# Tables in three parts, residuals ahead of low splits, earlier x1 loads: one change to a deformable-convolution and attention kernel

## The reference

```python
out = relu(bn(conv1x1(x, w1), g1, b1, m1, v1))               # 1024 -> 256 channels
offset = conv3x3(out, w_off, b_off)                          # 18 offsets a pixel
out = relu(bn(deform_conv3x3(out, offset, w2), g2, b2, m2, v2))  # 9 taps, 4 corners each
x = relu(bn(conv1x1(out, w3), g3, b3, m3, v3) + x)           # 256 -> 1024, residual
...
t, p, g = Wt @ x, Wp @ x, Wg @ x                             # 1024 -> 512 channels each
att = [sum(alpha_o * p**o * g) for o in 0, 1, 2]             # one number an image and order
y = sum(att_o * alpha_o * t**o)
z = Wz @ y                                                   # 512 -> 1024 channels
return (z - mean(z)) * rsqrt(var(z) + eps) * gn_w + gn_b + x
```

## Time and profile before

| what | us |
|---|---|
| median of 3 runs | 2401.27 |
| the three runs | 2401.27, 2420.3, 2396.08 |
| the profiled execution | 2397.66 |
| its span, first to last instruction | 2395.8 |
| busy: PE, PEld | 2252.3 (94%), 1860.6 (78%) |
| busy: DVE, ACT, POOL | 1575.6 (66%), 1248.5 (52%), 764.8 (32%) |
| DMA over the span | 684.76 MB, mean 286 GB/s |
| TensorE's mean granted clock | 0.974 |

### The profile page before, as it was taken

How to read it: one execution, slowest core, us unless ns; L and a number is a source line. 1 busy time by engine, 2 the same in 40 slices (tenths; PEclk the granted TensorE clock), 3 DMA queues, 4 the chain that set the end, 5 groups by cost and what they waited for, 6 DMA issues and landing times.

```text
span 2395.8 us, 29891 instructions
## 1 busy us (share of the span) xinstructions
PE 2252.3 (94%) x10252; PEld 1860.6 (78%) x10252; DVE 1575.6 (66%) x3177; ACT 1248.5 (52%) x2432; POOL 764.8 (32%) x706
## 2 busy tenths in 40 slices
PE   8999999998989999999999999999999999999960
PEld 6888887877867788888888887888778878887840
DVE  4213127667467888898888988898783324467774
ACT  6444444343455565666565655566553324456664
POOL 0100013324114554565567665766560000000000
PEclk9999999999989999999999999999999999999985
DMA  8998989999998898998899899999893111118679
GB/s 305 315 316 276 324 278 379 405 398 337 383 363 282 304 350 313 333 352 311 315 320 337 310 329 317 338 316 320 308 320 119 50 57 53 53 53 300 226 283 385
DMA packets 299040, 684.76 MB, mean 286 GB/s; under 512 B 28136, under 2 KB 102632, under 8 KB 292744
## 3 DMA queue, kind: packets, MB, share of 16 engines
q0 software_dynamic: 88048, 322.81, 38.4%
q1 hardware_dynamic: 175848, 266.26, 31.1%
q10 hardware_dynamic: 34992, 93.78, 10.5%
HBM read 443.86 MB, written 238.88 MB: 285 GB/s over the span
## 4 chain that ended last, share of the span: by engine, by line
PE 80%; DVE 7%; DMA 6%; issue 2%; SPq 2%; ACT 1%; POOL 1%; ACTq 0%; DVEq 0%; POOLq 0%
PE bank L197 22%; PE bank L199 22%; PE bank L198 22%; PE bank L1461 4%; PE bank L1462 4%; PE bank L1463 4%; PE bank L1479 1%; DMA xt<-x 1%; DMA vwide<-vb 1%; DVE a L1051 1%; DMA g<-vwide,tbl 1%; DVE z L1405 1%; POOL g L642 1%; DMA vone<-vb 1%; DMA xs<-x 1%
## 5 line engine op out<-in xcount | busy, mean ns | idle before, releaser
L642 POOL DMA_INDIRECT g<-vwide,tbl x512 | 581.2, 1135 | 651.0 <-DVE a L1035 324.2
L197 PE MATMUL bank<-x1h,wlh 128*128 128x512 f32 x1536 | 602.8, 392 | 4.9 <-DVE x1l L1294 3.0
L198 PE MATMUL bank<-x1l,wlh 128*128 128x512 f32 x1536 | 600.0, 391 | 1.3 <-issue 1.3
L199 PE MATMUL bank<-x1h,wll 128*128 128x512 f32 x1536 | 600.4, 391 | 0.9 <-issue 0.7
L1051 DVE SCALAR_TENSOR_TENSOR a<-g,tbl,a 128x256 f32<-128x256 f32 x1224 | 527.4, 478 | 43.0 <-DMA g<-vwide,tbl 37.8
L669 ACT ACTIVATE g<-g,tbl 128x256 f32<-128x256 f32 x1008 | 426.3, 498 | 241.2 <-DMA g<-vwide,tbl 130.7
L197 PEld LDWEIGHTS bank<-x1h,wlh 128*128 128x128 f32 x1536 | 288.8, 188 | 66.2 <-issue 5.8
L198 PEld LDWEIGHTS bank<-x1l,wlh 128*128 128x128 f32 x1536 | 288.9, 188 | 65.1 <-issue 4.3
L199 PEld LDWEIGHTS bank<-x1h,wll 128*128 128x128 f32 x1536 | 288.7, 188 | 63.0 <-issue 1.0
L753 ACT ACTIVATE vb<-bank 128x512 f32<-128x512 f32 (+1 forms) x320 | 173.0, 554 | 215.5 <-PE bank L1463 136.2
L1461 PE MATMUL bank<-w2h,o1h 128*128 128x512 f32 (+1 forms) x640 | 237.9, 372 | 5.4 <-ACT vb L753 4.1
(11 more groups left out here) (150 smaller groups left out, 3230.5 us busy)
## 6 DMA issues: line engine op xcount, KB each, us to landing
vwide<-vb SPq DMA_DIRECT2D x256, 256.0 KB, 4.2
vwide<-vb SPq DMA_DIRECT2D x112, 512.0 KB, 4.1
xf<-in_x SPq DMA_DIRECT2D x32, 1024.0 KB
x<-xf ACTq DMA_DIRECT2D x32, 1024.0 KB, 6.6
out<-z SPq DMA_DIRECT2D x128, 256.0 KB, 5.1
xin<-in_x ACTq DMA_DIRECT2D x54, 512.0 KB
t<-ts ACTq DMA_DIRECT2D x64, 256.0 KB
tb<-t POOLq DMA_DIRECT2D x16, 1024.0 KB, 5.4
```

The source lines that it names most:

```text
L197: nc.tensor.matmul(out, wh, xh, start=first, stop=False)
L198: nc.tensor.matmul(out, wh, xl, start=False, stop=False)
L199: return nc.tensor.matmul(out, wl, xh, start=False, stop=last)
L642: pool.indirect_dma_start(slot[:].rearrange("p a c -> p (a c)"), None, d["vwide"][img], bass.IndirectOffsetOnAxis(ap=at[:, i, tap(u), 0:1] ...
```

## The change

It has three parts. (1) `tables(i)` becomes `table_places`, `table_weights` and `table_entries`; for tables 0 to 2 the places are made where the whole table was, weights and entries in the next step, and SP stores the table a step later. In step 16 the parts of table 3 stand between the residual pairs. (2) In the seam the expansion uses four banks instead of two, all its pairs come ahead of the last taps, the low splits of weights 2 and 3 stand behind all residual pairs, three instead of four weights are split ahead of the projection, the rest one by one in its first groups, and a gather unit moves from point 5 to point 0 of step 16. (3) `adds_by` loses its cap, the eight XT slots in the z weights alternate between the two regions, and SP waits for the z tiles that free a slot instead of for all.

```diff
-            if s == 9 and point > 2 or 10 <= s < 15 and point or s == 15 and point in (1, 3) or s == 16 and point in (2, 3, 5):
+            if s == 9 and point > 2 or 10 <= s < 15 and point or s == 15 and point in (1, 3) or s == 16 and point in (0, 2, 3):
...
 def adds_by(x):
-    return max(0, min(64, max(x - 3, 3 * (x - 5) // 2), x + 4))
+    return max(0, min(64, max(x - 3, 3 * (x - 5) // 2)))
...
-    XT = XB + [m.put(f"xt{i}", [128, 2, NPX], at=at) for i, at in enumerate(early + [at + 4 * KB * i for at in (R1, G_AT) for i in range(4)])]
+    XT = XB + [m.put(f"xt{i}", [128, 2, NPX], at=at) for i, at in enumerate(early + [at + 4 * KB * i for i in range(4) for at in (R1, G_AT)])]
...
     def expansion_bank(n, o):
-        return BANK[(0, 1, 5, 6)[o % 4]] if n else BANK[o % 2]
+        return BANK[(0, 1, 5, 6)[o % 4]]
...
-                if s > 4 and s % 4 == 2:
-                    table((s - 6) // 4)
+                if s > 4 and s % 4 == 3:
+                    table((s - 7) // 4)
...
-                if j == len(XB) + len(early):
-                    sp.wait_ge(z_done, IMGS * ZT)
+                if j >= len(XB) + len(early):
+                    sp.wait_ge(z_done, IMGS * ZT - KIN + 2 * ((j - len(XB) - len(early)) // 2) + 2)
                 load_x1(ZT // 2 + j)
```

ScalarE, steps 16 and 17, the high splits ahead of chunk 0, and its groups:

```diff
-                if s == ALLC + 1:
-                    split_high(3)
-                    stage(6)
-                    table()
...
-                if tiles:
-                    v_evict(s - 1, 3)
                 if s >= ALLC:
                     x1_pair(0, 2 * (s - ALLC) + 1)
+                if tiles and s < ALLC:
+                    v_evict(s - 1, 3)
                 if s == ALLC:
                     split_high(2)
                     stage(5)
+                    split_high(3)
+                    stage(6)
+                if s == ALLC + 1:
+                    v_evict(ALLC - 1, 3)
+                    table()
...
-            for w in range(4, 8):
+            split_high(4)
+            for w in (5, 6):
                 split_high(w)
-                stage(w + 3)
+                stage(w + 2)
...
-                    if c == 0 and 1 <= q <= 5:
+                    if c == 0 and q <= 5:
                         split_high(7 + q)
-                        if q in (1, 2, 5):
-                            stage(10 + q if q < 3 else 13)
+                    if c == 0 and (q <= 3 or q == 6):
+                        stage(9 + q if q <= 3 else 13)
```

VectorE, in the front steps and ahead of chunk 0; the residual pairs stand where they stood:

```diff
-                for point in (2, 3):
-                    f_gather(s, point)
+                f_gather(s, 2)
+                if s % 4 == 2 and 6 <= s < ALLC:
+                    table_weights((s - 6) // 4)
+                f_gather(s, 3)
                 if s == ALLC:
                     offs(ALLC - 1)
+                    table_places(3)
...
-                if s == ALLC + 1:
-                    split_low(3)
...
-                    tables(3)
+                    table_weights(3)
...
-                    tables((s - 5) // 4)
+                    table_places((s - 5) // 4)
+                if s % 4 == 2 and 6 <= s < ALLC:
+                    table_entries((s - 6) // 4)
...
                 if s == ALLC:
+                    table_entries(3)
+                if s == ALLC + 1:
                     split_low(2)
+                    split_low(3)
...
-            for w in range(4, 8):
+            for w in range(4, 7):
                 split_low(w)
```

TensorE, in the expansion of chunk 0 and around it:

```diff
-                    at_least(pe, xr_done, KIN * n + o - 3 if n else o - 1)
+                    at_least(pe, xr_done, KIN * n + o - 3)
+                    if n == 0 and o == 2:
+                        pe.wait_ge(ys_done, ALLC)
+                    if n == 0 and o == 3:
+                        pe.wait_ge(off_done, ALLC)
...
-                if 1 <= s <= ALLC:
+                if 1 <= s < ALLC:
                     taps(s - 1, 3)
+                if s == ALLC + 1:
+                    taps(ALLC - 1, 3)
```

More of the change, by code:

```diff
@@ L1120, in o1_low, with chain @@
                         nc.vector.memset(o1_row(part[r], ROWS + 1).bitcast(fp32), 0.0).then_inc(halo_l, 1)
[L1122 to L1125, removed]
+            def chain(i, part):
+                count = sum(27 + (8 if WIDE[k // 2] < TAPS else 0) for k in range(i)) + (0, 13, 23)[part]
                 def link(ins):
@@ L1131, in link, with table_places @@
                     v.wait_ge(tab_chain, count)
+                return link
+            def table_places(i):
+                h, link = i % 2, chain(i, 0)
                 if i == 0:
                     v.wait_ge(tabc_in, 48)
-                at_least(v, tab_out, 16 * i)
                 v.wait_ge(off_done, 4 * i + 4)
@@ L1151, in tables, with table_weights @@
                 link(nc.vector.scalar_tensor_tensor(out=POS[:], in0=FLF[:], scalar=SIDE - 2.0, in1=POS[:], op0=ALU.is_le, op1=ALU.mult))
-                fy, fx = (FLF[:].rearrange("p t (k c) -> p t k c", c=2)[:, :, :, c] for c in range(2))
+            halves = [a[:].rearrange("p t o -> p (t o)")[:, n:n + HALF * TAPS].rearrange("p (t k) -> p t k", k=TAPS)
+                      for a in (GTT, POS, FLI) for n in (0, HALF * TAPS)]
+            ix, half, place, over, whole = halves[0:5]
+            fy, fx = (FLF[:].rearrange("p t (k c) -> p t k c", c=2)[:, :, :, c] for c in range(2))
+            def table_weights(i):
+                link = chain(i, 1)
                 hi, lo = (a[:].rearrange("p t (k c) -> p t k c", c=2) for a in (POS, GTT))
+                at_least(v, tab_out, 16 * i)
                 for c, (a, b) in enumerate(((lo, lo), (hi, lo), (lo, hi), (hi, hi))):
                     link(nc.vector.tensor_tensor(TAB[:, :, :, 2 + c], a[:, :, :, 0], b[:, :, :, 1], ALU.mult))
-                halves = [a[:].rearrange("p t o -> p (t o)")[:, n:n + HALF * TAPS].rearrange("p (t k) -> p t k", k=TAPS)
-                          for a in (GTT, POS, FLI) for n in (0, HALF * TAPS)]
-                ix, half, place, over, whole = halves[0:5]
-                ints = TAB[:].bitcast(i32)
                 link(nc.vector.tensor_scalar(half, fy, 0.5, 0.5, ALU.mult, ALU.add))
@@ L1166, in tables, with table_entries @@
                 link(nc.vector.tensor_tensor(place, place, over, ALU.subtract))
+            def table_entries(i):
+                img, link = i // 2, chain(i, 2)
+                w, ints = WIDE[img], TAB[:].bitcast(i32)
                 def index(column, taps, by_place, by_row, more):
@@ L1343, in _ @@
                         coefficients(0)
-                    if c == 0 and (1 <= q <= 5 or q == 7):
+                    if c == 0 and (q <= 5 or q == 7):
                         split_low(7 + q if q < 7 else 13)
```

## The result

The changed kernel took 2385.41 us in the median of 20 runs (2374.18 to 2406.2), the kernel before 2401.51 in 20 runs beside it (2396.08 to 2421.36). The ratio is 0.9924, 95% interval 0.9905 to 0.9944: 16 us faster by the medians, 18 by the ratio. The forecast was 2374, the range 2362 to 2388; so the time lies near the slow end of the range, and short of the border of 2377 at which 1% is reached. The profiled execution took 2379.09 us, 18.6 less than that of before.

The account below looks back on a forecast made before the run. TensorE was taken to bound the kernel, so time counts only where it waits or behind its last product. 5.4 + 4.4 + 6.5 - 1.5 + 10.0 = 24.8 off 2397.66 gave 2372.9, forecast as 2374, range 2362 to 2388.

Parts of the forecast that it names:

- rival B: Seam gives nothing: ScalarE's stage waits and later ReLUs eat what VectorE frees, o2's stall stays; 2385 us, chance 0.14.
- Front steps: Front end: making tables in parts shortens TensorE's stalls in steps 9 and 13; 5.4 us gained, between -2 and +12.
- The charge of 1.4 for steps 10 and 14: Front end: cost of table weights and entries reappearing one step later, 1.4 us, between 0 and 4.
- rival A: Front is held by DMA: what the tables free is waited for at V buffers; price 5.4 us, 2379, chance 0.18.
- Seam: Between front end and projection: first projection matmul at 694.3, 4.4 us earlier, between 0 and 8.
- Chunk 0: Splits beside the first projection: wait for o2's low half falls from 5.95 to 1.4; 6.5 us gained, between 2 and 8.
- three signs of being wrong: TensorE idle on vb above 8 us in steps 10 to 12, new acl wait, or end still 85 us behind the product.
- Adds: Adds of image 0 at 1.5 a tile: three more chunk ends carry that load; -1.5 us, between 0 and -5.
- End: Behind the last product: 14 of 16 x1 pair slots already full, fewer bytes left; 10.0 us gained, bounds 8.5 and 11.5.

Follow-up runs that it names:

- e3: Kernel before with only the seam part: expansion, last taps, table 3 and splits as changed; 2378.29 us, ratio 0.997 to the kernel before.
- e4: Kernel before with only the third part: uncapped adds, alternating slots, SyncE waiting for single z tiles; 2377.36 us, ratio 0.9968 to the kernel before.
- e8: Changed kernel with tables 0 to 2 made whole in one step again, their store a step earlier; 2369.07 us, ratio 0.9926 to the kernel before.
- e5: Changed kernel with table_weights moved behind the copies of y in steps 6, 10 and 14; 2367.73 us, ratio 0.9922 to the kernel before.
- e7: Changed kernel with both the edit of e5 and that of e6; 2367.57 us, ratio 0.9925 to the kernel before.
- e6: Changed kernel with ScalarE's loads of weights 5 and 6 moved behind the last V evictions and the table; 2367.94 us, ratio 0.9927 to the kernel before.
- e9: e6 with SyncE's first load of projection accumulators also ahead of the V stores of the last four tiles; 2386.62 us, ratio 0.9923 to the kernel before.
- e2: Kernel before with only tables 0 to 2 as changed, table 3, seam and pairs as before; 2383.05 us, ratio 0.9993 to the kernel before.
- e11: Changed kernel with the old cap on the adds of image 0 back; 2385.55 us, ratio 0.9936 to the kernel before.
- e1: Changed kernel unedited, run again for a second trace; 2366.76 us, ratio 0.9925 to the kernel before.
- e10: Changed kernel unedited, run for a third trace on another chip; 2386.48 us, ratio 0.993 to the kernel before.
- e12: Changed kernel with SyncE waiting for all z tiles ahead of the last eight pair slots, as before; 2389.85 us, ratio 0.9938 to the kernel before.

## Why the prediction was right, and where not

The range held and the sign was right; the size was 27 where 16 to 18 were measured. The number, 2385, is the one that rival B had, but B's reason is not: e3 shows that the seam alone gives 6.4. By the steps of the prediction:

- **Front steps, 5.4.** Mean of the fronts without the table part (before, e3, e4, e8) 262.8, with it 257.4: 5.4 in the traces. The sum was right by accident. Steps 9 and 13 gained 5.9 and 8.3 where I took 3.0 and 4.8. In step 13 two readings were off: the gather unit at the end of the table took 2.6 us (566.59 to 569.22) and not 3.3, which leaves a stall of 2.8 and not 3.7; and I added 2.7 of slow clock to it, while the granted clock stayed at 1.00 and the step was only 3.1 longer than a clean one. In before it had been 0.58 over the first 3.5 us behind the stall of 9.8. The charge of 1.4 for steps 10 and 14 failed: I wrote that the weights hide behind gathers that are late anyway, and did not name what is queued behind them, the copies of `y` for which TensorE waits. It cost 3.8 and 4.0 us, twice my upper end. But e5 and e7 take the waits for `y` away, and the front stays as long (257.3 and 256.6): these 4 us were not a loss that stands by itself. That speaks for rival A's mechanism, in steps 10 to 12 above all. In the runs the part is worth 1.3 to 1.7 us, and there A's price of nothing is nearer the mark than my 5.4.
- **Seam, 4.4.** 83.9 in the mean to 80.1: 3.8, by the chain I described. From ScalarE's first eviction of step 15, before to after, it is 84.4 to 80.1, which puts the first projection product where 694.3 did; the low splits end at 681.6, which is 688.4 with the 6.8 us of the front put back, where I had 688.0. ScalarE's wait of 5.75 at the stage load is the link I named; e6 shows that without it the projection starts 4.9 earlier and then waits about that much longer for accumulators.
- **Chunk 0, 6.5.** 123.4 to 119.6: 3.8. The wait for `o2l` went as forecast, from 5.95 to 1.44 or nothing, though in part because TensorE had lost time at the accumulators; e9, without that wait, has 2.8. What failed is the sentence on the accumulators, "landed at about 700, when the first projection group ends, so it is nothing, at most 3": they are wanted 7 to 8 us after the start and land 10 to 11 after it, a wait of 1.7 to 4.0 in the traces with the changed seam and the stage loads in place. SyncE issued this load 9.5 us ahead of the projection's start before the change and 5.6 behind it after. With the 6.8 us of the front put back it landed at some 704 and not at 700. A new wait on `acl` was also one of my three signs of being wrong, and it came.
- **Adds, -1.5.** z without early adds (before, e2, e3, e11) 367.2, with them 369.2: -2.0.
- **End, 10.0.** 78.0 to 68.9: 9.1, near my lower bound of 8.5; no run shows a rate that would make my upper bound of 11.5: DMA moved 410 GB/s in the 71 us behind 2319 in before, which makes 10.0 of the 4.1 MB I had counted. Two things were off and nearly cancel. From the first final add to the end 30.5 MB were left before, not 29.3, and 25.2 after, as I had it: 5.3 MB less, which at 0.41 MB/us is worth 12.9 us. But I took DMA to be full from the start, and in the first 8 us it moves 1.5 MB instead of 3.3, which gives 4.3 back. The 363 GB/s over 69.3 us is a mean: in the 54 us from 2316 on DMA moves 409, and 405 in the last 13 of them, with stores alone.

The sum was 24.8 against the profiled run; the terms as the traces have them make 5.4 + 3.8 + 3.8 - 2.0 + 9.1 = 20.1, with 1.7 for the tables, as e2's runs have it, 16.4. Measured were 16.1 (the medians of the result), 17.9 (e1) and 15.9 (e10). Of the 27 in the forecast 2.5 more were only the distance of the median of three from the profiled run.

## What to carry to other kernels

When work is moved past an engine's queue, write down for each new neighbour who waits for it: twice here a term was wrong by one waiting reader. `y` was not on the list at all; `acl` was, but its landing was put 4 us too early, because the load stands in SyncE's queue behind stores that had moved. In steps 10 to 12, at a DMA share of 1.05, a stall removed was in part a stall moved (waits for V buffers 5.3 us in after, 11.2 in e5); count bytes ahead of waits in such a stretch. The tail here, which is nothing but transfers, gave 9.1 us where 10.0 was forecast, but DMA had little to move at its start (193 GB/s over 8 us): 5.3 MB taken out of it gave 9 us and not 13. What allowed it was not the finer wait (2.5 us in e12) but the adds ahead of it in the queue (9.4 in e11).

## What the runs showed that was not expected

TensorE's own issue slows in places where nothing in the profile is waited for, in after with 0.3 to 1.6 us idle ahead of a matmul. TensorE's timeline of after:

```profile
1658.90 0.39 PE L197 MATMUL bank<-x1h,wlh 128*128 128x512 f32 x1 [0.34 <-issue]
1660.31 0.49 PE L198 MATMUL bank<-x1l,wlh 128*128 128x512 f32 x1 [1.03 <-issue]
1662.41 0.42 PE L199 MATMUL bank<-x1h,wll 128*128 128x512 f32 x1 [1.61 <-issue]
1663.12 0.78 PE L197 MATMUL bank<-x1h,wlh 128*128 128x512 f32 x1 [0.30 <-issue]
1664.53 0.59 PE L198 MATMUL bank<-x1l,wlh 128*128 128x512 f32 x1 [0.63 <-issue]
1666.65 0.59 PE L199 MATMUL bank<-x1h,wll 128*128 128x512 f32 x1 [1.53 <-issue]
```
One matmul in 0.7 to 2.1 us, then a granted clock of 0.50 over 1668 to 1672; the projection there is 1132.6 us, in e1 to e8 1117.9 to 1120.9. Such places stand in before, after and e9 to e12, mostly on other spots in each (1283, 1370 and 1674 in e9; 1430 in e12), and in no trace of e1 to e8. e1 to e8 ran on two chips and e9 to e12 on a third. In e9, whose projection takes 1141.5, they cost some 20 us, more than the change. DMA runs at shares of 0.8 to 1.0 around them, but in e1 it runs at 0.88 in the same stretch without harm. The cause was not tested.

Waits of the same length had different prices here, and the granted clock behind them differed with the price. Behind the 2.1 us wait for `y` at 586.74 the granted clock is 0.64 over 4 us, and step 14 is 4.0 longer than a clean step:

```profile
588.00:592.00 4.00, 4.00 (x13) 3.21 (x13) 3.97 (x11) 0.60 (x1) 1.47 (x3) 0.64 1.07 405
```
The same wait in step 10 of e11 leaves the clock at 1.00, and the step takes 41.7, 2.4 more than a clean one; in e9 both are the same. These are the wait in e11, the whole of that step, and step 13 of after, which waits 2.8 for `xl` and is 3.1 longer:

```profile
412.04 1.07 PE L1507 MATMUL bank<-sel,y 108*128 108x18 f32 x8 [2.07 <-DVE y L1216]
...
389.50:431.20 41.70, 39.63 (x202) 33.57 (x201) 32.64 (x78) 18.20 (x32) 13.18 (x12) 1.00 1.05 404
...
521.75:564.17 42.42, 39.61 (x201) 33.56 (x200) 32.56 (x76) 18.40 (x32) 17.41 (x12) 1.00 1.05 386
```
In step 10 of e2 and e6 the mean granted clock is 0.92, and that wait of 2.1 costs 5.5. What decides between them was not tested.
